# Centring on ScalarE instead of VectorE, and the chunk projection one slot earlier, in a two-layer attention, expert, state-space and ternary-FFN kernel

## The reference, cut to what matters

```python
x = x + L0_attn(xn) + L0_ffn(xn)              # xn = layernorm(x); x is 2048 x 128
xn = layernorm(x)                             # (x - m) / sqrt(v + 1e-5)
x = x + L1_attn(xn) + L1_ffn(xn)

def L1_attn(x):                               # state-space layer, 4 heads of 64, state 128
    z, x_ssm, B, C, dt_raw = split(rmsnorm(x) @ in_proj_w.T)
    xh = silu(causal_conv(x_ssm, 4 taps))
    dt = softplus(dt_raw + dt_bias); dA = exp(-exp(A_log) * dt)
    h = h * dA_t + dtx_t * B_t;  y_t = h . C_t            # a scan over the 2048 tokens
    return x + ((y + D * xh) * silu(z)) @ out_proj_w.T

def L1_ffn(x):                                # tlin(x, w, s) = (x @ w.T) * s
    h = silu(tlin(x, w1)) * tlin(x, w2)       # 128 -> 512
    h = gelu(tlin(h, h1)); h = gelu(tlin(h, h2))          # 512 -> 512, twice
    return tlin(h, w3)                        # 512 -> 128
```

## Time and profile before

| | us |
|---|---|
| median of 3 runs | 631.13 (630.4 to 631.23) |
| the profiled execution | 631.13 |
| its span | 629.4 |

### The profile page before, as it was taken

The page is one execution under the profiler, slowest core; times in us unless marked ns, Lnnn a source line. Parts: engine busy times, 40 slices in busy tenths (PEclk is TensorE's granted clock), DMA queues, the critical chain, the costliest instruction groups (busy, mean ns, idle before and its releaser), DMA issues.

```text
span 629.4 us, 11243 instructions
## 1 busy us (share of the span) xinstructions
PE 567.7 (90%) x3977; PEld 335.2 (53%) x3977; DVE 404.4 (64%) x1038; ACT 460.1 (73%) x614; POOL 150.1 (24%) x175
## 2 busy tenths in 40 slices
PE   4669999999999999999897799788789989989998
PEld 3324334444343433333334487366568868868887
DVE  7885865556444343475516654778898697697682
ACT  2378997998989999989666266578586765666563
POOL 2043222020110011002700745104032131131131
PEclk9779999999999999999989999999999999998999
DMA  7112002013422220210317221200000000000000
GB/s 231 25 37 68 2 1 68 1 41 105 170 102 94 93 86 1 76 61 8 110 25 225 65 75 39 80 1 1 1 1 2 2 17 1 2 18 1 1 18 18
DMA packets 31175, 31.00 MB, mean 49 GB/s; under 512 B 6912, under 2 KB 21024, under 8 KB 31120
## 3 DMA queue, kind: packets, MB, share of 16 engines
q1 hardware_dynamic: 29872, 27.71, 14.2%
q0 software_dynamic: 1248, 2.57, 1.1%
HBM read 13.44 MB, written 12.89 MB: 42 GB/s over the span
## 4 chain that ended last, share of the span: by engine, by line
PE 64%; DVE 24%; issue 5%; ACT 4%; SPq 1%; DMA 1%; POOL 1%; DVEq 0%; ACTq 0%; POOLq 0%
PE ps L1353 17%; PE ps L1334 9%; PE ps L92 5%; PE ps L94 5%; PE ps L93 4%; PE ps L1654 2%; PE ps L1430 2%; PE ps L1417 2%; DVE r L2398 2%; PE ps L1528 1%; PE ps L1251 1%; DVE r2r L2486 1%; DVE xn L2398 1%; DVE r L2495 1%; ACT r L970 1%
## 5 line engine op out<-in xcount | busy, mean ns | idle before, releaser
L970 ACT ACTIVATE r<-ps 128x1024 f32<-128x1024 f32 x272 | 258.3, 1034 | 33.6 <-PE ps L1334 31.1
L1353 PE MATMUL ps<-r 128*32 128x512 f32 (+3 forms) x1280 | 146.6, 544 | 1.9 <-POOL r L842 0.8
L842 POOL TENSOR_SCALAR_AFFINE_SELECT r<-r 128x512 f32<-128x512 f32 (+1 forms) x80 | 47.6, 598 | 217.8 <-ACT r L970 217.5
L1334 PE MATMUL ps<-r2r 32*128 32x512 f32 (+3 forms) x640 | 79.5, 450 | 8.7 <-DMA r2r<-r2r 4.4
L1334 PEld LDWEIGHTS ps<-r2r 32*128 32x128 f32 x640 | 34.7, 183 | 51.1 <-ACT r L970 20.8
L885 POOL TENSOR_TENSOR r<-r 128x512 f32<-128x512 f32 x16 | 22.1, 1384 | 135.7 <-ACT r L1168 135.7
L1353 PEld LDWEIGHTS ps<-r 128*32 128x32 f32 x1280 | 27.8, 108 | 42.2 <-issue 29.8
L94 PE MATMUL ps<-r2r 128*128 128x512 f32 (+1 forms) x104 | 39.1, 376 | 0.0
L93 PE MATMUL ps<-r2r 128*128 128x512 f32 (+1 forms) x88 | 33.4, 380 | 0.0
L820 POOL DMA_INDIRECT rows_by_expert<-r x16 | 17.7, 1109 | 63.5 <-DVE r L1991 59.6
L860 POOL DMA_INDIRECT rows_by_token<-r x23 | 24.1, 1049 | 18.4 <-issue 10.2
(11 more groups left out here) (401 smaller groups left out, 1224.0 us busy)
## 6 DMA issues: line engine op xcount, KB each, us to landing
rows_by_expert<-r SPq DMA_DIRECT2D x34, 258.0 KB, 2.4
r2r<-r2r SPq DMA_DIRECT2D x60, 64.0 KB, 2.0
r<-in_f_W SPq DMA_DIRECT2D x1, 2048.0 KB, 9.8
r<-rows_by_expert SPq DMA_DIRECT2D x23, 64.5 KB, 1.8
res<-in_x SPq DMA_DIRECT2D x4, 256.0 KB, 4.3
r<-in_g_h1T SPq DMA_DIRECT2D x1, 1024.0 KB, 5.9
r<-in_g_h2T SPq DMA_DIRECT2D x1, 1024.0 KB, 8.2
r<-rows_by_token SPq DMA_DIRECT2D x4, 256.0 KB, 3.8
```

Of the source, the lines that this page charges most:

```text
L842: pool.affine_select(blk, blk, pattern, ALU.is_ge, nothing, base=0, channel_multiplier=-1).then_inc(s_msk, 1)
L970: act.activation(probs[:, n % PBUFS, :, :], ps[:, b:b + 2, :], ACT.Exp).then_inc(s_exp, 1)
L1334: m = pe.matmul(ps[:, 2 * (n % SBUFS) + h, at:at + TB - query], kst[32 * j:32 * j + 32, group, P * kt:P * kt + P], qst[32 * j:32 * j + 32, ...
L1353: m = pe.matmul(ps[32 * j:32 * j + 32, 6, query:TB], vp[:, kt, group, :], probs[:, (2 * v + j // 2) % PBUFS, j % 2, at:at + TB - query], s ...
```

## The change

Two things. First, `centred(b)` leaves VectorE's program and enters ScalarE's, as Identity with scale `inverse` and bias `offset`; `offset` is -mean x inverse, a new small operation of VectorE at the end of `normalised(q)`, and `s_inv` tells ScalarE of it. ScalarE runs `centred(0)` between `taken(1)` and `taken(2)`, `centred(1)` after `taken(2)`, `centred(2)` after `taken(3)` and `centred(3)` between `z_gates(2)` and `z_gates(3)`. On VectorE `middle_weights_low(1)` moves ahead of `xs_low(3)`, where `centred(0)` was. Second, in the loop `projected(i)` goes from slot 2i + 3, ahead of `state(i + 1)`, to slot 2i + 2, ahead of `chunk(i + 2)`; on VectorE `chunk_added` and `finished` go to the head of their odd slot, ahead of `chunk_started` and the taps. For the last chunk but one (slot 30) `projected` is issued although there is no further `chunk`.

```diff
--- before.py
+++ after.py
@@ -305,6 +305,7 @@
             [w[:, a:b] for a, b in ((0, 256), (256, 512), (512, 640), (640, 768), (640, 772))] for w in (inh, inl))
         roots = small[:, 32:64].rearrange("p (q a i) -> p q a i", q=NB, a=2)
         inverse = small[:, 64:96].rearrange("p (q a i) -> p q a i", q=NB, a=2)
+        offset = small[:, 96:112].rearrange("p (q i) -> p q i", q=NB)
         btd = r2[:, 16388:18500].rearrange("p (i c) -> p i c", i=NT)
         z2 = r1[:, 0:4096].rearrange("p (m t) -> p m t", m=MI)
         xc = r1[:, 8192:12312].rearrange("p (m b t) -> p m b t", m=MI, b=NB)
@@ -443,6 +444,7 @@
         s_xth = sem("convolution_tanh")
         s_diag = sem("in_proj_rows_scaled")
         s_inh = sem("in_proj_high")
+        s_inv = sem("layer1_inverse_roots")
         s_halo = sem("convolution_edges_ready")
         s_cva = sem("convolution_last_tap")
         s_cvt = sem("convolution_sums")
@@ -1056,6 +1058,13 @@
                     act.activation(dst[:, b * TB:b * TB + TB], ps[:, proj_bank(what, b), :], ACT.Copy
                                    ).then_inc(s_pja, 1)
 
+            def centred(b):
+                act.wait_ge(s_inv, b + 1)
+                for i in range(TPB):
+                    t = TPB * b + i
+                    act.activation(xn[:, t, :], res[:, t, :], ACT.Identity, bias=offset[:, b, i:i + 1],
+                                   scale=inverse[:, b, 0, i:i + 1]).then_inc(s_xn2, 1)
+
             def z_gates(b):
                 for k in range(2):
                     act.wait_ge(s_pj, proj_done(f"z{k}", b))
@@ -1114,7 +1123,9 @@
             states_read(2)
             xs_high(3)
             taken(1)
+            centred(0)
             taken(2)
+            centred(1)
             tokens_read(3)
             states_read(3)
             for m in range(MI):
@@ -1122,8 +1133,10 @@
             xn_high(0)
             z_gates(1)
             taken(3)
+            centred(2)
             xn_high(1)
             z_gates(2)
+            centred(3)
             z_gates(3)
             act.wait_ge(s_dta, 1)
             act.activation(ea, alog, ACT.Exp).then_inc(s_dtb, 1)
@@ -1701,11 +1714,12 @@
 
             def chunk_units(s):
                 if s % 2:
-                    if s > 1:
+                    state(s // 2)
+                else:
+                    if s:
                         projected(s // 2 - 1)
-                    state(s // 2)
-                elif s // 2 + 1 < NCH:
-                    chunk(s // 2 + 1)
+                    if s // 2 + 1 < NCH:
+                        chunk(s // 2 + 1)
 
             pe.wait_ge(s_cvr, 2 * NB)
             for o in range(1, FO):
@@ -2366,12 +2380,8 @@
                     t = TPB * q + i
                     dve.tensor_scalar(xs[:, TPB * (q % 2) + i, :], res[:, t, :], mv[:, t, 0:1], inverse[:, q, 1, i:i + 1],
                                       ALU.subtract, ALU.mult).then_inc(s_xs, 1)
-
-            def centred(b):
-                for i in range(TPB):
-                    t = TPB * b + i
-                    dve.tensor_scalar(xn[:, t, :], res[:, t, :], mv[:, t, 0:1], inverse[:, b, 0, i:i + 1],
-                                      ALU.subtract, ALU.mult).then_inc(s_xn2, 1)
+                dve.scalar_tensor_tensor(offset[:, q], mv[:, TPB * q:TPB * q + TPB, 0], -1.0, inverse[:, q, 0],
+                                         ALU.mult, ALU.mult).then_inc(s_inv, 1)
 
             def middle_weights_low(k):
                 dve.wait_ge(s_fhi, FO + 2)
@@ -2435,13 +2445,9 @@
                 measured(q)
                 normalised(q)
             middle_weights_low(0)
-            centred(0)
+            middle_weights_low(1)
             xs_low(3)
             taps_added(0)
-            centred(1)
-            centred(2)
-            centred(3)
-            middle_weights_low(1)
             middle_weights_low(2)
             middle_weights_low(3)
             dve.wait_ge(s_pja, act_read("D1", NB - 1))
@@ -2566,6 +2572,10 @@
                         if o == 0:
                             down_added(b - 1)
                     else:
+                        if s >= 3:
+                            chunk_added(s // 2 - 1)
+                        if o == 1 and b:
+                            finished(b - 1)
                         if s // 2 + 1 < NCH:
                             chunk_started(s // 2 + 1)
                         if b < NB - 1 and o in (1, 3):
@@ -2573,10 +2583,6 @@
                         elif b < NB - 1 and o == 5:
                             for m in range(MI):
                                 gated_c(b + 1, m)
-                        if s >= 3:
-                            chunk_added(s // 2 - 1)
-                        if o == 1 and b:
-                            finished(b - 1)
                     if o >= FO and b < NB - 1:
                         up_gated(b + 1, o - FO)
             state_carried(NCH - 1)
```

## The result

The kernel after the change took 647.24 us (median of four executions; one of them, at 875.23, was disturbed, the other three lie from 646.36 to 647.25) against 630.76 for the kernel before on the same chip: a ratio of 1.0256, 95% interval 1.0236 to 1.0276, slower. I had forecast 643.4 and 637 to 647: the direction and the mechanism hold, the forecast is 3.8 us short, and the median lies just above the upper end of the range.

The account below looks back on a forecast made before the run. TensorE held 64% of the chain and VectorE 24%, with ScalarE nearly as late between the layers. 631.1 + 3.3 (part A) + 7.3 (part B) + 1.7 (clock) = 643.4 us, range 637 to 647.

Parts of the forecast that it names:

- Part A: Between the layers, `centred` moves from VectorE to ScalarE, which lacks idle time for it: +3.3 us, bounds +0.6 to +5.1.
- part B: In the loop, `projected(i)` one slot earlier makes TensorE wait for VectorE's gate product: +7.3 us before the clock's share.
- the six slots named: Slots 2, 6, 10, 14, 18 and 22, where TensorE was to wait some 2.8, 1.2 and 3.4 us.
- Rivals 1 to 3: ScalarE hides `centred`: 640.7 (0.15); loop stalls only move existing waits: 634.4 (0.08); gaps and clock falls vanish: 625.4 (0.06).
- rival 1: Between the layers, ScalarE hides `centred` at lower-bound activation cost, loop stalls stand: 640.7 us; chance 0.15.
- block 0, first half: Loop, slot 2: stall of 2.81 less the existing 1.35 gap, 1.5 us, plus 1.7 for a new clock fall.
- slots 6, 14, 22: Loop: TensorE stalls 1.23 us in each, with no gap behind to absorb them, 3.7 us in all.
- blocks 1 and 2, first half: Loop, slots 10 and 18: stalls of 3.41 less existing gaps of 2.82, 0.6 us each, 1.2 in all.
- block 3: End of the loop: 0.26 us in slot 28 and a risk in slot 26, taken as 0.9 in all.
- the clock: TensorE's granted clock falls behind block 0's longer gap, +1.7 us; blocks 1 and 2 keep the falls they have.
- the reversed order that I had half priced: Slot 26: GpSimd's product starts before VectorE's line 2515, costing about 0.8 us, of which half was kept.
- The rival of 650: Loop: the port lock hits lines 2515 and 2528 in every block 3 slot, more clock falls: 650 us; chance 0.06.

Follow-up runs that it names:

- The filled kernels: Idle TensorE matmuls ahead of long loop waits, added to the changed kernel (636.03 us, ratio 1.0106) and to the kernel before (624.91 us, 0.9939).
- tensor_order_only: Kernel before with only `projected(i)` moved to slot 2i+2 on TensorE, VectorE's order unchanged: 650.29 us, ratio 1.0259.
- vector_order_only: Kernel before with only `chunk_added` and `finished` moved ahead of `chunk_started` on VectorE: 639.62 us, ratio 1.0101.
- taps_filled: Kernel before with VectorE's m = 1 taps moved from slot 3 to 4 and 11 idle matmuls in TensorE's wait between layers: 621.47 us, ratio 0.9843.
- taps_filled_slots: taps_filled plus the `projected` move on TensorE and the `chunk_added` and `finished` move on VectorE: 650.50 us, ratio 1.0259 to the kernel before.
- centring_only: Kernel before with only `centred` moved from VectorE to ScalarE, loop order unchanged: 634.12 us, ratio 1.0002.
- taps_filled_centring: taps_filled plus `centred` moved from VectorE to ScalarE: 623.56 us, ratio 0.9875 to the kernel before.

## Why the prediction was right, and where it was short

**What bounds, and the order of the parts: right.** Part A slows the stage because ScalarE decides, part B makes stalls at exactly the six slots named, and the waits of the earlier trace rows vanish. Rivals 1 to 3 fell: the activations are not cheap, the stalls do not disappear, and the gaps of blocks 1 and 2 close only by being replaced by larger ones.

**Part A: forecast +3.3, measured +2.94.** The activation takes 0.585 us, not 0.46, but four in a row take 1.77, so they follow each other every 0.39 instead of 0.36: 0.4 us more over 16. The idle time that they fill, 2.0, was right. What I had too small is what comes back where the idle time closes: the other operations of the stretch take 14.6 - 6.1 = 8.5 us instead of 9.44, so 0.9 and not 0.3. And the 0.1 for the new VectorE operation is not on the path. These errors of +0.4, -0.6 and -0.1 make the -0.3 or so. My bounds for part A (+0.6 and +5.1) left out the last two terms; with them they are +0.4 and +4.9, and rival 1 is 640.5. The Trainium skill, page "ScalarE: Activation LUTs", section "What ACT_TABLE_LOAD costs", has 186 ns + 0.833 ns per column, about 93 ns more for each of two column operands, and 93 ns of overlap with the next, an estimate of 0.386 us from one to the next; this case's trace agrees in the distance (0.39 us), not in the duration of one (0.585).

**Part B and its clock: forecast +9.0, measured +12.87.** TensorE's arrival at a slot, counted from `chunk(1)`, minus the same in before, gives the delay so far: slot 6 +3.72 (490.90 - 1.58 - 456.58 against 485.07 - 456.05), slot 8 +5.41, slot 14 +7.28, slot 16 +8.97, slot 22 +10.92, slot 24 +12.61, the end +12.87. Their differences, split at the stalls:

| step | forecast | measured |
|---|---|---|
| block 0, first half, with its fall of the clock | 1.5 + 1.7 | 3.7 |
| slots 6, 14, 22 | 3 x 1.23 = 3.7 | 3 x 1.7 = 5.1 |
| blocks 1 and 2, first half | 2 x 0.6 = 1.2 | 1.9 + 2.0 |
| block 3 | 0.9 | 0.3 |

- The term that failed is the clock, at +1.7: "Blocks 1 and 2 have their fall already and keep it." They have a deeper one. In before the clock is 0.61 over 4.34 us, a loss of 1.7; in after it is 0.50 over 5.42, a loss of 2.7, behind a wait that grew from 2.82 to 3.67 us. Block 0's fall was mis-sized too: 0.50 over 5.00 us. The filled kernels measure the clock over the loop: 7.55 against 3.17 us, 4.4 more, where I had put 1.7; by block +2.3 in block 0 (forecast 1.7) and +1.0 in each of blocks 1 and 2 (forecast 0). That is 2.7 of the 3.9 us missing.
- The stalls of slots 6, 14 and 22 are 1.58 instead of 1.23, and with the overlap that a waiting matmul loses (0.71 instead of 0.60) cost 1.7. I had taken the arrival from a program in which `projected` still stood in the slot before; without it TensorE comes earlier to its wait: from the start of the last `up` product ahead of slot 5 to its wait in slot 6 it takes 6.26 us instead of 6.55, while the gate product ends 7.79 us behind that start, against 7.78. That is another 1.4 us.
- The stalls of 3.67 instead of 3.41 in slots 10 and 18 are the same effect: from the start of the last matmul of slot 8's `chunk` TensorE takes 4.77 us to slot 10 instead of 5.04, and the gate product ends 8.38 us behind that start, against 8.45.
- Block 3 went the better way, 0.3 instead of 0.9: GpSimd starts at 612.80, 0.14 us behind VectorE's line again, so the reversed order that I had half priced did not come. Where it came, in tensor_order_only, the wait was 1.13 us.
- I said that the time which moving `chunk_added` ahead saves, 0.2 to 0.4 us per slot, is used up by the later `chunk`. The chains of 7.8 and 8.4 us, which hardly changed, bear that out, and without the move slots 10 and 18 wait 0.43 us longer. But I had seen only a part of what it does: with slot 26 it saves 1.9 us in this kernel, and by itself it costs 8.0. My sum used neither number.

**The rival of 650** names two more falls of the clock, 3.4 us. The clock did cost 2.7 us more than forecast, but by longer and deeper falls and not by more of them; the rival's stalls in block 3 did not come.

## What to carry to other kernels

- An engine that executes in order pays for a wait at the place where the wait stands. Moving a consumer ahead to its producer's slot frees nobody unless someone waits for the consumer. Compare arrival and producer slot by slot, and subtract from the arrival what the move itself takes away.
- A stall costs its length minus the next wait of the same engine that already exists, plus the clock behind it. In this loop a wait that grew from 2.8 to 3.7 us cost 1.9 us and not 0.9, about 1.0 of it clock.
- The better edit was in the cause of the old gap: the three taps of m = 1, moved out of VectorE's chain to `middle_low(b, 3)`, gave 0.9814 [0.9779, 0.9850]. Where a gap can't be closed, idle matmuls in it give back the clock (7.55 and 3.17 us here).

## What was not expected of the hardware

- The same TensorE wait of 2.62 or 2.63 us between the layers was followed by a fall of the granted clock in 7 of the 11 profiles that have it and by none in 4, being one of these. The price was 1.0 to 4.1 us on a stage of 36.4 us. In the three profiles with the wait filled there was no fall behind it. A later wait, some 31 us behind the first transposes, is 2.94 us long without part A and was followed by no fall in the four profiles that have it (before, vector_order_only, taps_filled, taps_filled_slots); with part A it is 1.95 or 1.97 us, and a fall followed in centring_only and taps_filled_centring, none in after. A comparison of two profiles, and of a few executions, can hide a change of 3 us behind this.
- In the loop the length of a wait did not decide either. After and both other kernels with its order of TensorE fell behind all three long waits (3.67 to 4.39 us); taps_filled_slots, whose base has no such gap, fell behind its waits of 4.38 and 2.75 us and not behind those of 3.67, and with `projected` behind `chunk` one wait of 3.42 had a fall and the other none. A price for the clock is therefore good to a few us only, even where the wait is known exactly.
